# Expert loop of a gated attention and mixture-of-experts kernel: both groups of TensorE transposes put between the gate product and the linear product

## The chip, the cores and the metric

The kernel runs on one core of a Trainium2 chip. The metric is the device time of one execution in microseconds (us). The kernel before takes 871.43 us, the median of three runs (871.41 to 871.66). The profile is of one more execution, which took 875.14 us; its traced span is 873.4 us.

TensorE is called PE here, and its loading of the stationary operand PEld. VectorE is DVE, ScalarE is ACT, GpSimd is POOL, and SP issues plain loads and stores.

## The reference

The input has 8 sequences of 256 tokens with 512 features. Two residual steps are computed: a sigmoid attention against a context, and then a mixture of 16 experts, of which each token uses 4. All of it is float32.

```
x = x + tanh(g_xattn) * attention(layernorm(x), ctx, ctx)
x = x + tanh(g_ffn) * ffn(layernorm(x))

ffn:  t = rms_norm(x) * norm_w
      G = softmax over the 4 largest of (t @ gate_w.T + gate_b), zero elsewhere
      h = t @ w1[e].T + b1[e]                 # 512 -> 2 * 512, for each expert e
      a = min(h[even], 7);  b = clip(h[odd], -7, 7)
      act = a * sigmoid(1.702 * a) * (b + 1)
      y = act @ w2[e].T + b2[e]               # 512 -> 512
      out = x + sum over e of G[e] * y
```

## The kernel before, in words

The first stage, up to about 205 us, does the attention and the routing. It leaves the normed token rows in HBM (`t_rows`) and, for each expert, a list of its tokens with their gates. The expert loop then works through blocks of 128 listed rows. There are 75 blocks with the numbers 0 to 74; blocks 0 to 3 are written out in straight code, and blocks 4 to 74 run in the loops of `over_experts` (line 274). An expert has about five blocks. The change touches the loop's blocks alone.

For block `g` the work is this:

- POOL gathers the 128 rows from `t_rows` into `xg` (`gather`, line 463, indirect DMA on line 472). There is one `xg` for all loop blocks, so the gather waits until PE has turned the rows that were in it (`xt_mm`, line 469).
- PE turns the rows with four 128x128 transposes into the PSUM bank `ps_x` (`turn_rows`, line 1190; the transposes are on line 1187, in the helper `turn`).
- ACT copies `ps_x` to `xt_hi` (line 657) once PE has also finished the linear product of the block before, which still reads `xt_hi`; DVE writes the remainder to `xt_lo` (line 955).
- PE multiplies: `gate_product` (12 matmuls of 512 columns) and `linear_product` (12 more). Each operand is held as a high and a low part, hence three matmuls for each of the four slices of 128. All products have line 1211, in the helper `product`.
- ACT and DVE form the activated rows `hid` (DVE lines 980, 984, 989, 993, 996 and ACT line 673).
- PE turns `hid` into `ps_h` (`turn_hidden`, line 1200), ACT and DVE split it into `ht_hi` and `ht_lo` (lines 663 and 961), and PE does the third product (`down`, line 1215, 12 matmuls).
- DVE adds the bias (`y_sb`, line 968). POOL scales the rows by their gates (`y_out`, line 485) and adds them to the output by an indirect DMA (line 489).

The blocks overlap. In one pass of the loop with the number `g`, PE does the gate and linear products of block `g`, turns the hidden rows of block `g - 1`, turns the input rows of block `g + 1`, and does `down` of block `g - 1`. In one pass POOL scales and sends the rows of one block and then gathers the rows of a later one: `add_rows(before)`, `gather(g + 2)`. Its passes run one block behind those of PE, so the gather that a pass of PE needs is the last thing that POOL did, and it is issued behind the scaling (line 485) and the adding (line 489) of finished rows.

In the first three passes of each expert ACT and DVE also split the next expert's weights into high and low parts, two pieces of 1024 columns each pass: ACT line 563, DVE line 889 (`w_lo`). SP loads each piece of the raw weights as soon as its place is free.

The order on every engine is the order of the code; semaphores join the engines.

Of the kernel before, what the change touches and what calls it, by code (L numbers as in the profile page):

```python
# [43 lines left out]
def gated_attention_moe(nc, x, ctx_k, ctx_v, gates_in, norm_w, gate_wt, gate_b, w_cat, b_cat, out):  # L44
# [24 lines left out]
    with ExitStack() as ctx:  # L69
# [176 lines left out]
        def wait_past(eng, s, value):  # L246

            if not isinstance(value, int) or value > 0:
                eng.wait_ge(s, value)  # L249
# [6 lines left out]
        def rows_of(g):  # L256

            if not isinstance(g, int):
                return xg
            return xg_second if g in (1, 4) else xg_third if g == 2 else xg  # L260
# [841 lines left out]
        def _(pe):  # L1102
# [81 lines left out]
            def turn(dst, src):  # L1184
                for k in range(KT):
                    c = slice(k * P, (k + 1) * P)
                    ins = pe.transpose(dst[:, c], src[:, c], ident_r[:])  # L1187
                return ins

            def turn_rows(g):  # L1190
                if isinstance(g, int) and g in (1, 4):
                    pe.wait_ge(second_in, DMA * (1 if g == 1 else 2))
                elif isinstance(g, int) and g == 2:
                    pe.wait_ge(third_in, DMA)
                else:
                    pe.wait_ge(gathered, DMA * ({0: 1, 3: 2}.get(g, g - 2) if isinstance(g, int) else g - 2))
                wait_past(pe, xt_ready, g)
                turn(ps_x[:].bitcast(F32R), rows_of(g)).then_inc(xt_mm, 1)

            def turn_hidden(g):  # L1200
                pe.wait_ge(hid_ready, g + 1)
                pe.wait_ge(ht_ready, g + 1)
                turn(ps_h[:].bitcast(F32R), hid_r).then_inc(ht_mm, 1)

            def product(dst, hi, lo, wh, wl, col, step):

                n = 0
                for k in range(KT):
                    c = slice(col + k * step, col + k * step + 512)
                    for lhs, rhs in ((hi, wh), (hi, wl), (lo, wh)):  # L1210
                        ins = pe.matmul(dst[:], lhs[:, k, :], rhs[:, c], start=n == 0, stop=n == 3 * KT - 1)  # L1211
                        n += 1
                return ins

            def down(g, parity):
                pe.wait_ge(ht_ready, g + 2)
                wait_past(pe, y_ready, g)
                product(ps_y, ht_hi, ht_lo, w_hi[parity], w_lo[parity], W1COLS, H).then_inc(y_mm, 1)

            def gate_product(g, parity):  # L1220
                pe.wait_ge(xt_ready, g + 1)
                wait_past(pe, a_ready, g)
                product(ps_a, xt_hi, xt_lo, w_hi[parity], w_lo[parity], 0, 2 * I).then_inc(a_mm, 1)

            def linear_product(g, parity):
                wait_past(pe, b_read, g)
                product(ps_b, xt_hi, xt_lo, w_hi[parity], w_lo[parity], I, 2 * I).then_inc(b_mm, 1)

            def block(e, parity, g, before, first, share):
                if first:  # L1230
                    pe.wait_ge(hi_ready, NPW * e + NP1)
                    pe.wait_ge(lo_ready, NPW * e + NP1)
                gate_product(g, parity)
                turn_hidden(before)
                linear_product(g, parity)
                turn_rows(g + 1)
                down(before, 1 - parity if first else parity)
                if first:
                    pe.wait_ge(hi_ready, NPW * (e + 1))
                    pe.wait_ge(lo_ready, NPW * (e + 1))  # L1240
# [62 lines left out]
            turn_rows(4)  # L1303

            last = over_experts(pe, block)
            keep_clock_up(2)
            turn_hidden(last)
# [42 lines left out]
```

## Time and profile before

| | |
|---|---|
| median of the runs shown | 871.43 us |
| the profiled execution | 875.14 us, span 873.4 us |
| PE busy | 832.9 us, 95% of the span |
| DVE / POOL / ACT busy | 67% / 58% / 37% |
| granted PE clock, mean | 0.985 of full |
| chain of waits that ended last, PE's share | 73% |

The table is read from the top down: PE is busy nearly throughout, and the chain of work that ended last lies mostly on its matmuls. An average over the span does not say how much room there is before a transfer becomes late; that is read from single passes.

### The profile page before, as it was taken

The numbers are of one execution on the slowest core, as the hardware profiler recorded it, in microseconds if no ns is written. First come the engines' busy times: TensorE is split into PE (matmuls) and PEld (weight loads), VectorE is DVE, ScalarE is ACT, GpSimd is POOL, SyncE is SP. The second block draws the span as 40 slices with busy tenths as digits, with TensorE's granted clock in tenths as the row PEclk, the third lists the DMA queues.
The fourth block names the chain that finished last, engine by engine and source line by source line (L and its number), as shares of the span: only waits on it lengthen the run. The fifth ranks groups of instructions, "written<-read, shape, count | busy, mean of one in ns | idle before, by whom it ended". The sixth has DMA issues, their size and how long they took to land.

```text
span 873.4 us, 14819 instructions
## 1 busy us (share of the span) xinstructions
PE 832.9 (95%) x3836; PEld 639.6 (73%) x3837; DVE 582.0 (67%) x1137; ACT 320.4 (37%) x464; POOL 505.1 (58%) x523
## 2 busy tenths in 40 slices
PE   4999899988899999999999999999999999999994
PEld 2554455766788888888888888888888888888883
DVE  4465677675578677767768778585766858585652
ACT  3555576531243324233333433332332333332111
POOL 0033345654467666667666677676675757676563
PEclk9999999999999999999999999999999999999998
DMA  5653576517377676537667757474554747443323
GB/s 181 229 171 121 169 222 211 163 58 185 106 194 202 170 173 167 135 89 194 154 145 197 216 128 204 94 194 102 146 146 71 194 91 200 102 97 51 72 48 48
DMA packets 51077, 127.50 MB, mean 146 GB/s; under 512 B 8240, under 2 KB 12336, under 8 KB 51056
## 3 DMA queue, kind: packets, MB, share of 16 engines
q1 hardware_dynamic: 32048, 87.35, 30.3%
q0 software_dynamic: 19008, 39.93, 25.7%
q8 instruction: 7, 0.11, 0.0%
q14 instruction: 14, 0.11, 0.0%
HBM read 96.25 MB, written 31.00 MB: 146 GB/s over the span
## 4 chain that ended last, share of the span: by engine, by line
PE 73%; DMA 1%; issue 0%; POOL 0%; ACT 0%; DVE 0%; POOLq 0%; DVEq 0%; ACTq 0%
PE bank L1211 68%; PE bank L1187 5%; DMA xg<-t_rows,gather_idx 1%; PE bank L1247 0%; POOL out_rows L549 0%; ACT y_last L723 0%; DVE y_sb L968 0%; POOLq L452 0%; DVEq L249 0%; POOLq L552 0%; POOLq L548 0%; ACTq L722 0%
## 5 line engine op out<-in xcount | busy, mean ns | idle before, releaser
L663 ACT ACTIVATE ht_hi<-bank 128x512 fp32r<-128x512 f32 x75 | 44.9, 599 | 352.7 <-PE bank L1187 345.5
L485 POOL TENSOR_SCALAR y_out<-y_sb,add_gate 128x512 f32<-128x512 f32 x71 | 155.7, 2192 | 16.2 <-DVE y_sb L968 15.0
L489 POOL DMA_INDIRECT out_rows<-y_out,add_idx x73 | 119.6, 1638 | 64.6 <-POOL y_out L485 37.8
L472 POOL DMA_INDIRECT xg<-t_rows,gather_idx x72 | 86.0, 1195 | 74.3 <-issue 38.6
L1211 PE MATMUL bank<-w_hi_even,xt_hi 128*128 128x512 f32 x312 | 126.1, 404 | 2.2 <-DVE xt_lo L955 2.0
L439 POOL DMA_INDIRECT list_rows<-entry,place x64 | 64.6, 1010 | 108.7 <-DVE place L875 91.0
L1211 PE MATMUL bank<-w_hi_even,xt_lo 128*128 128x512 f32 x312 | 123.4, 395 | 0.0
L1211 PE MATMUL bank<-w_lo_even,xt_hi 128*128 128x512 f32 x312 | 122.5, 393 | 0.0
L961 DVE TENSOR_TENSOR ht_lo<-bank,ht_hi 128x512 fp32r<-128x512 f32 x75 | 51.9, 691 | 103.2 <-ACT ht_hi L663 103.1
L1211 PE MATMUL bank<-w_hi_odd,xt_hi 128*128 128x512 f32 x288 | 115.5, 401 | 1.1 <-DVE xt_lo L955 1.1
L1211 PE MATMUL bank<-w_hi_odd,xt_lo 128*128 128x512 f32 x288 | 113.0, 392 | 0.0
L1211 PE MATMUL bank<-w_lo_odd,xt_hi 128*128 128x512 f32 x288 | 112.2, 390 | 0.0
L984 DVE SCALAR_TENSOR_TENSOR up_b<-bank,bias 128x512 f32<-128x512 f32 x75 | 51.8, 691 | 69.7 <-PE bank L1211 65.1
L1116 PE MATMUL bank<-k_sb,q 128*128 128x512 f32 x128 | 61.4, 625 | 11.2 <-DMA k_sb<-in_ctx 7.9
L955 DVE TENSOR_TENSOR xt_lo<-bank,xt_hi 128x512 fp32r<-128x512 f32 x76 | 52.5, 691 | 27.5 <-ACT xt_hi L657 26.6
L1211 PEld LDWEIGHTS bank<-w_hi_even,xt_hi 128*128 128x128 f32 x312 | 59.1, 189 | 13.8 <-issue 2.6
L1211 PEld LDWEIGHTS bank<-w_hi_even,xt_lo 128*128 128x128 f32 x312 | 59.1, 189 | 13.3
L673 ACT ACTIVATE up_s<-up_a 128x512 f32<-128x512 f32 x75 | 47.4, 632 | 56.3 <-DVE up_a L980 56.3
L1211 PEld LDWEIGHTS bank<-w_lo_even,xt_hi 128*128 128x128 f32 x312 | 59.2, 190 | 11.5
L1211 PE MATMUL bank<-w_hi_even,ht_hi 128*128 128x512 f32 x156 | 64.8, 415 | 0.0
L657 ACT ACTIVATE xt_hi<-bank 128x512 fp32r<-128x512 f32 x76 | 45.5, 598 | 47.5 <-PE bank L1187 45.9
L1211 PEld LDWEIGHTS bank<-w_hi_odd,xt_lo 128*128 128x128 f32 x288 | 54.0, 188 | 12.1
(168 smaller groups left out, 1678.7 us busy)
## 6 DMA issues: line engine op xcount, KB each, us to landing
raw<-in_w SPq DMA_DIRECT2D x96, 512.0 KB
bias<-in_b SPq DMA_DIRECT2D x16, 768.0 KB
k_sb<-in_ctx SPq DMA_DIRECT2D x8, 512.0 KB, 3.8
v_sb<-in_ctx_t SPq DMA_DIRECT2D x8, 512.0 KB
t_rows<-t_sb SPq DMA_DIRECT2D x8, 512.0 KB
out_rows<-base SPq DMA_DIRECT2D x8, 512.0 KB
x_sb<-in_x SPq DMA_DIRECT2D x7, 512.0 KB
t_rows<-zeros SPq DMA_DIRECT2D x1, 2048.0 KB, 9.4
```

The source lines that it names most:

```text
L439: pool.indirect_dma_start(out=list_rows, out_offset=bass.IndirectOffsetOnAxis(ap=place[:, j, k:k + 1].bitcast(U32), axis=0), in_=entry[:, ...
L472: pool.indirect_dma_start(out=xg[:].bitcast(F32), out_offset=None, in_=t_rows, in_offset=bass.IndirectOffsetOnAxis(ap=gather_idx[:], axis= ...
L485: pool.tensor_scalar(y_out[:], y_sb[:], add_gate[:, 0:1], None, ALU.mult).then_inc(yo_ready, 1)
L489: pool.indirect_dma_start(out=out, out_offset=bass.IndirectOffsetOnAxis(ap=add_idx[:], axis=0), in_=y_out[:], in_offset=None, compute_op=A ...
L657: act.activation(xt_hi[:].rearrange("p k t -> p (k t)"), ps_x[:], ACT.Copy).then_inc(xt_hi_ready, 1)
L663: act.activation(ht_hi[:].rearrange("p k t -> p (k t)"), ps_h[:], ACT.Copy).then_inc(ht_hi_ready, 1)
L673: act.activation(up_s[:], up_a[:], ACT.Sigmoid, scale=ALPHA).then_inc(sg_ready, 1)
L955: dve.tensor_tensor(xt_lo[:].rearrange("p k t -> p (k t)"), ps_x[:], xt_hi[:].rearrange("p k t -> p (k t)").bitcast(F32), ALU.subtract).th ...
L961: dve.tensor_tensor(ht_lo[:].rearrange("p k t -> p (k t)"), ps_h[:], ht_hi[:].rearrange("p k t -> p (k t)").bitcast(F32), ALU.subtract).th ...
L984: dve.scalar_tensor_tensor(out=up_b[:], in0=ps_b[:], scalar=1.0, in1=bias[:, parity, I:2 * I], op0=ALU.add, op1=ALU.add).then_inc(b_read, 1)
L1116: ins = pe.matmul(ps_s[n % 3][:], q[:, j, n * P:(n + 1) * P], k_sb[:, j, :], start=j == 0, stop=j == J - 1)
L1211: ins = pe.matmul(dst[:], lhs[:, k, :], rhs[:, c], start=n == 0, stop=n == 3 * KT - 1)
```

## The change

In the loop's pass the four transposes of the next block's input rows move from behind the linear product to ahead of it. They then stand directly behind the four transposes of the hidden rows.

```
                 gate_product(g, parity)
                 turn_hidden(before)
+                turn_rows(g + 1)
                 linear_product(g, parity)
-                turn_rows(g + 1)
                 down(before, 1 - parity if first else parity)
```

Nothing else is changed: DVE, ACT, POOL and SP have the same instructions in the same order, and every wait stays with its instruction.

On PE before, this is the seam between the gate product and the linear product. `hid_r` is the hidden block, `w_hi`, `w_lo`, `xt_hi` and `xt_lo` are the two parts of the weights and of the turned input.

```order
L1211 MATMUL bank<-w_lo_even,xt_hi 128x512
L1211 MATMUL bank<-w_hi_even,xt_lo 128x512
L1187 MATMUL bank<-ident_r,hid_r 128x128 x4
L1211 MATMUL bank<-w_hi_even,xt_hi 128x512
L1211 MATMUL bank<-w_lo_even,xt_hi 128x512
```

Before, the gathered rows `xg` are turned behind the linear product; the register instruction belongs to the wait for the gather. `ht_hi` marks the start of `down`.

```order
L1211 MATMUL bank<-w_lo_even,xt_hi 128x512
L1211 MATMUL bank<-w_hi_even,xt_lo 128x512
L1196 REGISTER_ALU
L1187 MATMUL bank<-ident_r,xg 128x128 x4
L1211 MATMUL bank<-w_hi_even,ht_hi 128x512
L1211 MATMUL bank<-w_lo_even,ht_hi 128x512
```

After the change the first seam holds both groups, and the wait for the gather stands between them, ahead of the whole linear product.

```order
L1211 MATMUL bank<-w_lo_even,xt_hi 128x512
L1211 MATMUL bank<-w_hi_even,xt_lo 128x512
L1187 MATMUL bank<-ident_r,hid_r 128x128 x4
L1196 REGISTER_ALU
L1187 MATMUL bank<-ident_r,xg 128x128 x4
L1211 MATMUL bank<-w_hi_even,xt_hi 128x512
L1211 MATMUL bank<-w_lo_even,xt_hi 128x512
```

After the change nothing stands between the linear product and `down`.

```order
L1211 MATMUL bank<-w_lo_even,xt_hi 128x512
L1211 MATMUL bank<-w_hi_even,xt_lo 128x512
L1211 MATMUL bank<-w_hi_even,ht_hi 128x512
L1211 MATMUL bank<-w_lo_even,ht_hi 128x512
L1211 MATMUL bank<-w_hi_even,ht_lo 128x512
```

So 12 matmuls of 512 columns and one wait have changed places in each of the 71 passes of the loop, and the number of instructions is the same.

## Rows read from the trace of the kernel before

**Rows 1.** The page: chain that ended last, by line.
```profile
PE bank L1211 68%; PE bank L1187 5%; DMA xg<-t_rows,gather_idx 1%; PE bank L1247 0%; POOL out_rows L549 0%; ACT y_last L723 0%; DVE y_sb L968 0%; POOLq L452 0%; DVEq L249 0%; POOLq L552 0%; POOLq L548 0%; ACTq L722 0%
```

**Rows 2.** PE's waits: us in total, times, longest.
```profile
PE bank L1187 <- DMA xg<-t_rows,gather_idx: 2.5, 1, 2.5
```

**Rows 3.** Timeline of PE, one pass: start us, us, what, count.
```profile
439.10 0.46 PE L1187 MATMUL bank<-ident_r,xg 128*128 128x128 f32 x4
439.39 0.46 PE L1211 MATMUL bank<-w_hi_even,ht_hi 128*128 128x512 f32 x1
442.22 0.39 PE L1211 MATMUL bank<-w_hi_even,xt_hi 128*128 128x512 f32 x1
444.95 0.45 PE L1187 MATMUL bank<-ident_r,hid_r 128*128 128x128 f32 x4
445.24 0.46 PE L1211 MATMUL bank<-w_hi_even,xt_hi 128*128 128x512 f32 x1
448.09 0.46 PE L1187 MATMUL bank<-ident_r,xg 128*128 128x128 f32 x4
```

**Rows 4.** Timeline of PE ahead of the loop: `down` straight behind a linear product.
```profile
192.06 0.39 PE L1211 MATMUL bank<-w_hi_even,ht_hi 128*128 128x512 f32 x1
194.55 0.39 PE L1211 MATMUL bank<-w_hi_even,ht_lo 128*128 128x512 f32 x1
```

**Rows 5.** Timeline of PE ahead of the loop: the second of two groups of transposes.
```profile
180.34 0.51 PE L1187 MATMUL bank<-ident_r,xg_third 128*128 128x128 f32 x4
180.69 0.24 PE L1282 MATMUL bank<-carry,ones_r 128*128 128x16 f32 x1
```

**Rows 6.** Timeline of POOL in the pass of rows 3.
```profile
441.54 1.33 POOL L472 DMA_INDIRECT xg<-t_rows,gather_idx  x1 [0.81 <-issue]
```

**Rows 7.** Timeline of ACT and DVE in the same pass.
```profile
439.59 0.60 ACT L657 ACTIVATE xt_hi<-bank 128x512 fp32r<-128x512 f32 x1 [0.55 <-PE bank L1187]
441.28 0.69 DVE L993 SCALAR_TENSOR_TENSOR up_u<-up_s,up_b 128x512 f32<-128x512 f32 x1
442.01 0.69 DVE L996 SCALAR_TENSOR_TENSOR hid<-up_a,up_u 128x512 f32<-128x512 f32 x1
```

**Rows 8.** DMA in the window 444.8 to 445.0: POOL's queue, packets, MB, share.
```profile
q0 software_dynamic: 3, 0.00, 0.8%
```

**Rows 9.** Longest wait for a gather: chain, PE's timeline, DMA in 221.3 to 221.4.
```profile
213.43 8.26 DMA xg<-t_rows,gather_idx
...
216.33 0.46 PE L1211 MATMUL bank<-w_hi_even,xt_hi 128*128 128x512 f32 x1
221.74 0.54 PE L1187 MATMUL bank<-ident_r,xg 128*128 128x128 f32 x4 [2.45 <-DMA xg<-t_rows,gather_idx]
222.11 0.47 PE L1211 MATMUL bank<-w_hi_even,ht_hi 128*128 128x512 f32 x1
226.53 0.40 PE L1211 MATMUL bank<-w_hi_odd,xt_hi 128*128 128x512 f32 x1
...
q0 software_dynamic: 1, 0.00, 0.6%
```

**Rows 10.** Windows: busy us (x count) by engine, PE clock, DMA share, GB/s.
```profile
222.90:226.20 3.30, 3.30 (x9) 2.54 (x8) 2.41 (x4) 0.01 (x1) 1.11 (x2) 0.51 0.31 79
```

**Rows 11.** POOL's gathers and PE's hidden transposes, first and last of 43 close passes.
```profile
243.80 1.36 POOL L472 DMA_INDIRECT xg<-t_rows,gather_idx  x1 [0.83 <-issue]
247.23 0.29 PE L1187 MATMUL bank<-ident_r,hid_r 128*128 128x128 f32 x2
...
792.03 1.31 POOL L472 DMA_INDIRECT xg<-t_rows,gather_idx  x1 [0.81 <-issue]
795.42 0.29 PE L1187 MATMUL bank<-ident_r,hid_r 128*128 128x128 f32 x2
```

**Rows 12.** The same two for one of the 27 other passes.
```profile
620.15 1.02 POOL L472 DMA_INDIRECT xg<-t_rows,gather_idx  x1 [1.63 <-PE bank L1187]
624.68 0.29 PE L1187 MATMUL bank<-ident_r,hid_r 128*128 128x128 f32 x2
```

More of the change, by code:

```diff
@@ L1234, in block @@
                 turn_hidden(before)
+                turn_rows(g + 1)
                 linear_product(g, parity)
-                turn_rows(g + 1)
                 down(before, 1 - parity if first else parity)
```

## The prediction

> **What bounds the kernel now.** I read the chain of work that ended last first. It lies for 68% of the span on the products of line 1211 and for 5% on the transposes; a gather has 1% [rows 1]. The list of PE's waits comes next: in 70 of the 71 passes PE waits for no gather, and in one it waits 2.5 us [rows 2]. So PE sets the pace. The timeline of one pass gives it [rows 3]: gate product from 442.22, hidden transposes at 444.95, linear product at 445.24, row transposes at 448.09, and the same transposes one pass earlier at 439.10. A pass is 448.09 - 439.10 = 8.99 us. The question is what comes due earlier. The row transposes do: their place moves from 448.09 to about 445.24, by the 2.85 us of the linear product.
>
> **How close the gather is.** POOL issued this pass's gather from 441.54 to 442.87 [rows 6]. Its queue still moved packets in the window 444.8 to 445.0 and none after; narrowing the window puts the last one at 444.88 [rows 8]. From the issue's end to the landing are 2.0 us. The one long wait shows what follows: the last packet of that gather passed between 221.3 and 221.4 (narrowed: 221.33), and PE's transposes began at 221.74, so 0.41 us lie between landing and PE [rows 9]. The rows are thus usable at 444.88 + 0.41 = 445.29. Before, they are needed at 448.09: 2.8 us of room. After, they are needed at 445.24: none.
>
> I did the same for all gathers with a pass behind them, 70 beyond the long one. In 43 the place of the hidden transposes plus 0.29 us lies less than 0.5 us behind the landing (mean 0.26). The first and the last are [rows 11]: issue ends at 245.16 and 793.34, landings by narrowed windows at 247.27 and 795.37, transposes possible at 247.52 and 795.71. Over these the landing takes 1.9 to 2.3 us, mean 2.07. In the other 27 there is 0.9 us or more; [rows 12] has 624.68 + 0.29 against 623.19. The close ones are mostly the passes in which DVE also splits weights.
>
> **Does the room move with PE?** A wait only costs once if POOL runs freely, and each time if the gather is tied to PE. In the close passes the gather's end is 5.22 us ahead of the row transposes almost without exception. It takes 1.33 us there and 1.02 elsewhere [rows 6, 12], and ends 0.17 us behind the end of `hid` on DVE (442.70) [rows 6, 7]. I read this as POOL being held while DVE computes `up_u` and `hid`. Those follow ACT's copy to `xt_hi`, which began 0.20 us behind the row transposes before (439.39 to 439.59) [rows 3, 7]. After the change that copy follows the end of the linear product instead, because it waits for it too. Hence the gather's end stays 442.87 - 439.39 = 3.48 us behind the end of the last PE work ahead of `down`, whichever that is. A late PE makes the gather late, and the wait comes back in each close pass.
>
> The Trainium skill, page "Advanced Engine Details and Errata", section "GPSIMD Details", says that GpSimd shares a read and a write interface with VectorE and conflicts with VectorE instructions that have two SBUF inputs. That fits `up_u` and `hid`, which have two, and speaks for the tie; without it the gather would end after 1.02 us, 0.31 us earlier, which is the first rival below.
>
> **The sum, part by part.** Against the profiled execution's 875.14 us (span 873.4).
>
> 1. *Repeated wait, 43 passes.* Counted from the end of the linear product: gather ends at 3.48, lands at 3.48 + 2.07 = 5.55, usable at 5.96. PE gets there by `down` (2.72 to 2.84), gate (444.95 - 442.22 = 2.73) and hidden transposes (0.29) at 5.74 to 5.86. It waits 0.10 to 0.22 us. Then come 0.35 us of row transposes and 2.85 us of linear product: the pass takes 9.16 us against 8.99, +0.18. Times 43: +7.7. With landings of 1.9 and 2.3 us throughout it would be +0.5 and +17.6.
> 2. *Quiet passes, 27.* `down` loses the transposes in front of it. Behind transposes it takes 442.22 - 439.39 = 2.83 us [rows 3]; straight behind a linear product 12 matmuls take 2.49 / 11 x 12 = 2.72 [rows 4]. That gains 0.11. The second group of transposes costs 0.35 us instead of 0.29, since its first weight load no longer hides behind a long matmul [rows 5]: loses 0.06. Net -0.05, times 27: -1.4. Bounds: 0, and -0.12 if the second group costs nothing extra.
> 3. *The first pass of the loop.* The gather lands at 221.33 whatever PE does: it was issued long before, and it is the raw weights that it shares the DMA engines with. Before, the linear product ran from 216.33 to 219.1, ahead of that wait [rows 9]; it now comes behind it, +2.80. PE then idles from 216.33 to 221.74, 5.4 us instead of 2.6. After the 2.45 us wait the clock fell to half (0.51 of full in 222.9 to 226.2) and `down` took 226.53 - 222.11 = 4.42 us instead of 2.8 [rows 9, 10]. A longer idle time starts that stretch earlier at most; two matmuls more at 0.43 instead of 0.23 us make 0.3 to 0.4. I take +3.1. Bounds 2.8, and 5.2 if all twelve run at half clock.
> 4. *Nothing on the other engines.* DVE's linear rows start 0.3 us later in a pass, but into a gap of 0.2 to 0.3 us ahead of `xt_lo`; `xt_lo` is ready 1.5 us behind the linear product and the gate product needs it at 2.7. `hid` ends 3.3 us behind it and is needed at 5.5. If that cover went, each 0.1 us would cost 7 us over 71 passes; I cost it at 0.
>
> Sum: 7.7 - 1.4 + 3.1 = +9.4. The profiled execution would take 884.5, 3.7 us above its median as now: 871.43 + 9.4 = 880.8 us.
>
> **The rivals.**
>
> *No repeated wait (same).* POOL is not tied to `hid` but runs ahead once PE has been delayed. For it: the change moves `xt_mm` forward, for which POOL waits in the quiet passes [rows 12], and a pass 0.3 us longer puts `up_u` behind the gather's start; then the gather takes 1.02 us and the wait vanishes. Against: in the close passes the gather starts 0.26 us inside `up_u` [rows 6, 7], and a pass lengthened by 0.18 leaves it there. Only terms 2 and 3 would be left, with 70 quiet passes instead of 27: 3.1 - 3.5 to 3.1 - 1.4, that is 871.0 to 873.1, middle 872.1.
>
> *Faster.* The unbroken run of 36 matmuls is worth more than I allow: no penalty for the second group and 0.12 us gained in each of 70 passes, with landings early enough. It needs the landing to take under 1.85 us, or the tie to be gone. Time: -8.4 + 2.8 = -5.6, 865.8 us. It decides once the gain per pass exceeds 2.8 / 70 = 0.04 us with no waits. Against it stands the mean room of 0.26 us, less than the 0.41 us from landing to PE.
>
> *Later landings (slower still).* The landing takes longer when its packets meet others: the gather beside the first raw weights took 8.3 us from issue to landing [rows 9], and three or four of the quiet passes' had 2.3 to 2.5 us from its end. With 0.19 us more in each close pass the sum grows by 8.2: 889.0 us.
> The Trainium skill, page "DMA: Bandwidth & Descriptors", section "Anatomy of one DMA — SWDGE (gpsimd) path", gives about 2.0 us plus the bytes over 436 GB/s for a transfer issued by GpSimd. For the 256 KB of a gather that would be an estimate of 2.6 us; the trace has 2.0 to landing and 2.41 to PE's start. Counted from the end of the issue, the page would give this rival's time. By the trace alone it is the less likely.
>
> That the change does not do what it says is no rival: the order on PE shows the moved matmuls in every loop body.
>
> **How the numbers follow.** Forecast (tied gather, 880.8): 0.59, own range 875 to 886 from landings of 1.95 to 2.2 us. No repeated wait: 0.16. Faster: 0.11. Later landings: 0.14. A measurement of this kernel can tell about 0.2% (1.7 us) from no change. Faster holds the third case and a little of the second: 0.13. Same holds most of the second: 0.12. Slower holds the rest, 0.75. The range runs from 872, which keeps half of the second case, to 889.
>
> **What would show it.** In the changed kernel's list of PE's waits, line 1187 on the gather should have some 40 waits, 0.1 to 0.3 us each and 5 to 10 us together, besides one of 5.4 us that ends near 221.7. Passes in which weights are split should take 9.1 to 9.2 us, quiet ones 8.9 to 9.0. `down` should have 0.23 us behind its first matmul, and the gather should still end 0.17 us behind `hid`. The forecast is wrong if the close passes stay at 8.9 to 9.0 us, or if gathers there take 1.02 us.

## The result and the profile after

The changed kernel takes 882.60 us (median of five runs, 882.20 to 886.01); the kernel before took 871.43 us beside it. The ratio is 1.0125, with a 95% interval of 1.0106 to 1.0144: slower by some 11 us. The forecast was 880.8 us. The profiled execution of the changed kernel took 886.01 us (span 884.3), 3.4 us above its median, as that of before lies 3.7 above its own, so the two spans may be compared: 884.3 - 873.4 = 10.9 us.

The page and the list of PE's waits, to be read against [rows 1, 2]. A wait's row gives us in total, times, longest.

```profile
PE 836.7 (95%) x3836; PEld 646.2 (73%) x3837; DVE 583.3 (66%) x1137; ACT 320.1 (36%) x464; POOL 506.3 (57%) x523
PE bank L1211 6%; PE bank L1187 1%; DMA xg<-t_rows,gather_idx 0%; POOL out_rows L549 0%; PE bank L1247 0%; ACT y_last L723 0%; DVE hid L996 0%; DVE up_u L993 0%; DVE y_sb L968 0%; ACT xt_hi L657 0%; DVE up_b L989 0%; DVE xt_lo L955 0%; POOLq L279 0%; DVEq L249 0%; POOLq L552 0%
PE bank L1187 <- DMA xg<-t_rows,gather_idx: 7.3, 10, 3.9
```

The shares of this chain sum to 7%: it could be followed back over the last stretch alone, and its percentages are no measure. It still has one new thing in it: `hid`, `up_u` and `xt_hi` now stand on a chain that ends at PE. The waits for a gather have become ten: the long one of the first pass and nine more, 3.3 us together. But ten are not all. A wait of a few tenths disappears under the overlapping ends of the matmuls, so I read it as the distance from the hidden transposes to the row transposes. Without a wait that is 0.29 to 0.30 us. In 34 passes it is longer, by 9.85 us together.

One such pass on PE, to be read against [rows 3]: start us, us, what, count.

```profile
443.58 0.45 PE L1187 MATMUL bank<-ident_r,hid_r 128*128 128x128 f32 x4
444.09 0.55 PE L1187 MATMUL bank<-ident_r,xg 128*128 128x128 f32 x4
444.48 0.47 PE L1211 MATMUL bank<-w_hi_even,xt_hi 128*128 128x512 f32 x1
...
447.28 0.39 PE L1211 MATMUL bank<-w_hi_even,ht_hi 128*128 128x512 f32 x1
...
450.00 0.39 PE L1211 MATMUL bank<-w_hi_even,xt_hi 128*128 128x512 f32 x1
...
452.72 0.46 PE L1187 MATMUL bank<-ident_r,hid_r 128*128 128x128 f32 x4
453.15 0.53 PE L1187 MATMUL bank<-ident_r,xg 128*128 128x128 f32 x4
```

ACT, POOL and DVE ahead of its end, to be read against [rows 6, 7]:

```profile
447.54 0.60 ACT L657 ACTIVATE xt_hi<-bank 128x512 fp32r<-128x512 f32 x1 [0.88 <-PE bank L1211]
449.32 1.49 POOL L472 DMA_INDIRECT xg<-t_rows,gather_idx  x1 [0.81 <-issue]
449.23 0.69 DVE L993 SCALAR_TENSOR_TENSOR up_u<-up_s,up_b 128x512 f32<-128x512 f32 x1
449.95 0.69 DVE L996 SCALAR_TENSOR_TENSOR hid<-up_a,up_u 128x512 f32<-128x512 f32 x1
```

The loop goes round: the linear product ends near 447.28, ACT copies `xt_hi` behind it (its releaser is now line 1211 and no longer 1187), `hid` ends at 450.64, the gather at 450.81, 0.17 behind it, and 2.34 us later PE may turn the rows. From hidden transposes to hidden transposes the pass is 452.72 - 443.58 = 9.14 us.

A pass without a wait is 8.91 us on average (this one 8.88), and in it the three products stand close together (answers to [rows 4, 5]):

```profile
243.41 0.46 PE L1187 MATMUL bank<-ident_r,hid_r 128*128 128x128 f32 x4
243.71 0.51 PE L1187 MATMUL bank<-ident_r,xg 128*128 128x128 f32 x4
244.05 0.46 PE L1211 MATMUL bank<-w_hi_odd,xt_hi 128*128 128x512 f32 x1
...
246.85 0.39 PE L1211 MATMUL bank<-w_hi_odd,ht_hi 128*128 128x512 f32 x1
...
249.57 0.39 PE L1211 MATMUL bank<-w_hi_odd,xt_hi 128*128 128x512 f32 x1
```

`down` takes 249.57 - 246.85 = 2.72 us, and the second group of transposes 244.05 - 243.71 = 0.34.

The first pass of the loop, with the long wait (answers to [rows 9, 10]); the windows give busy us (x count) of PE, PEld, DVE, ACT, POOL, then PE's clock, DMA share and GB/s:

```profile
219.04 0.46 PE L1187 MATMUL bank<-ident_r,hid_r 128*128 128x128 f32 x4
223.44 0.75 PE L1187 MATMUL bank<-ident_r,xg 128*128 128x128 f32 x4 [3.94 <-DMA xg<-t_rows,gather_idx]
223.99 0.76 PE L1211 MATMUL bank<-w_hi_even,xt_hi 128*128 128x512 f32 x1
```
```profile
219.00:223.40 4.40, 0.50 (x5) 0.31 (x3) 1.29 (x2) 1.23 (x2) 0.00 (x0) 0.84 0.83 263
223.50:228.60 5.10, 5.10 (x15) 4.13 (x16) 0.00 (x0) 0.00 (x0) 1.55 (x4) 0.50 0.16 51
228.60:231.80 3.20, 3.20 (x14) 2.57 (x14) 2.48 (x5) 0.60 (x1) 0.00 (x0) 0.97 0.01 3
```

From the start of the hidden transposes PE does nothing else for 4.4 us, 3.94 of them listed as a wait. Then row transposes and linear product run at 0.50 of the full clock, the lower of its two levels (1.2 of 2.4 GHz).

All passes of the loop, measured from hidden transposes to hidden transposes (the first interval is the loop's first pass, the last, of 6.8 us, goes to the products behind the loop):

| | before | after |
|---|---|---|
| first interval | 13.32 us | 15.49 us |
| passes with a wait | none | 34, mean 9.23 us |
| passes without | 69 of 8.99 us | 35, mean 8.91 us |
| sum from first to last | 640.20 us | 648.06 us |

By kind: 34 x (+0.24) = +8.2 us, 35 x (-0.075) = -2.6, the first interval +2.2, the last +0.1. Together +7.9. The other 3 us of the span lie ahead of the loop, whose first hidden transposes come at 219.04 instead of 215.94. The change touches nothing there, and in the traces of the runs below this start lies anywhere between 211.8 and 218.8 us. So the trace shows 7.9 us that the change can have caused; the timed runs say some 11. A second trace of the changed kernel, at the end of the next section, has +7.4 in the loop and a start at 216.28. Where the other 3 us of the timed difference lie is not shown.

### The profile page after: what moved, and what is told of

Its sections match the earlier page's. It is cut to its first block and busy times, and to the rows that moved or that the text cites. A ratio compares the mean times of both kernels' runs of the same rounds, so it can differ in the third digit from the quotient of the medians.

```text
span 884.3 us, 14819 instructions
## 1 busy us (share of the span) xinstructions
PE 836.7 (95%) x3836; PEld 646.2 (73%) x3837; DVE 583.3 (66%) x1137; ACT 320.1 (36%) x464; POOL 506.3 (57%) x523
## 5 line engine op out<-in xcount | busy, mean ns | idle before, releaser
L485 POOL TENSOR_SCALAR y_out<-y_sb,add_gate 128x512 f32<-128x512 f32 x71 | 158.3, 2230 | 24.2 <-DVE y_sb L968 23.9
L1211 PEld LDWEIGHTS bank<-w_hi_odd,xt_hi 128*128 128x128 f32 x288 | 54.0, 188 | 11.6 <-issue 1.5
L1211 PEld LDWEIGHTS bank<-w_lo_odd,xt_hi 128*128 128x128 f32 x288 | 54.2, 188 | 10.1
```

The source lines that it names most:

```text
L485: pool.tensor_scalar(y_out[:], y_sb[:], add_gate[:, 0:1], None, ALU.mult).then_inc(yo_ready, 1)
```

## The experiments

My theory: of the 11 us about 3.5 come from the first pass of the loop and some 7 from gathers that are tied to PE through `hid`. What ties them is POOL's own work ahead of the gather, above all the scaling of `y_out`, which DVE holds up. Rivals: the new order costs something by itself, or the whole price is the first pass. All ratios are to the kernel before on the same chip; 0.001 is 0.87 us. There it took 872.51, 876.48 or 875.92 us, while the expectations reckon from 871.4; so their times are to be read as differences from that.

### The first pass alone, from both sides

```
-                turn_rows(g + 1)
+                late = isinstance(e, int) and e == 0
+                if not late:
+                    turn_rows(g + 1)
                 linear_product(g, parity)
+                if late:
+                    turn_rows(g + 1)
```

This is the changed kernel with the old order in the passes of expert 0. The traces show that this is the first pass of the loop alone: the next one already has the length of the other order.

> The changed kernel, but in the passes of expert 0 (the first of them is the one with the long wait for the gather) the row transposes stand behind the linear product as before. Theory 1 (three terms: the first pass costs about 2.2 to 3.1 us, some 34 passes wait again and again, the quiet ones gain 0.07 each): 2 to 3.5 us less than the changed kernel's 882.6, so 879.1 to 880.6. Rival (most of the loss sits in the first pass and the clock that falls behind it; the repeated waits are given back elsewhere): 872 to 875.

Measured: 878.96 us, ratio 1.0085 (1.0060 to 1.0111), which is +7.4 us. The first interval is 12.54 us, and 38 later passes have a wait, of 9.19 us on average. The loop of this trace is 644.87 us, +4.7, again some 3 us less than the timed runs say. By either measure most of the price is in the later passes.

The reverse, the kernel before with the new order in expert 0 alone (the same lines with `if late` and `if not late` exchanged):

> The kernel before, with the row transposes ahead of the linear product in expert 0's passes alone. Theory 1: only the first pass's term, +2 to +3.5 us: 873.5 to 875. Rival (the first pass costs nothing because the later start of the linear product is made up in the passes behind it): 871.4.

Measured: 879.22 us, ratio 1.0040 (1.0019 to 1.0061), +3.5 us. All passes but the first are 8.98 to 9.00 us. The first interval is 17.38:

```profile
217.96 0.46 PE L1187 MATMUL bank<-ident_r,hid_r 128*128 128x128 f32 x4
224.03 0.75 PE L1187 MATMUL bank<-ident_r,xg 128*128 128x128 f32 x4 [5.61 <-DMA xg<-t_rows,gather_idx]
```
```profile
218.40:223.40 5.00, 0.02 (x1) 0.00 (x0) 1.29 (x2) 1.23 (x2) 0.00 (x0) 0.97 0.94 307
223.70:229.00 5.30, 4.97 (x15) 4.00 (x16) 0.00 (x0) 0.00 (x0) 1.51 (x4) 0.50 0.18 49
```

Here the wait is about as long as the prediction gave it (5.61 us listed, 5.4 forecast), and the half clock covers the linear product behind it. The two runs add up to the whole of the change: 7.4 + 3.5 = 10.9 us. That they meet to the tenth is chance, since each is known to about 2 us only; by the plain medians they are 6.5 and 2.7.

### The gather ahead of the scaling

```
             def block(e, parity, g, before, first, share):
-                add_rows(before)
                 gather(g + 2)
+                add_rows(before)
```

In the changed kernel POOL issues the gather first and only then scales and adds.

> The changed kernel, but POOL issues the gather of a pass ahead of scaling and adding the finished rows, not behind. Theory 1: the gather lands some 5 us before it is needed, the 34 repeated waits (9.9 us in the profile, 8.2 us of longer passes) vanish and these passes become quiet ones of 8.91 us; left is the first pass: 882.6 - 8.2 - 34 x 0.07 = 872.0 (871 to 874). Rival (the second group of transposes and the changed timing on DVE lengthen the pass, the gather is only what the wait is booked on): 878 or more, with the time booked on another wait.

Measured: 879.93 us, ratio 1.0099 (1.0078 to 1.0119). In time, that missed. The passes show why: with few exceptions they are now 8.91 to 8.92 us, as the theory wants, but near 741 there are some of 11.56, 9.88, 9.12, 9.29 and 9.29 us. POOL, DVE and PE there:

```profile
741.61 0.18 POOL L480 CAST add_idx<-lists 128x1 uint32 x1 [4.20 <-DMA out_rows<-y_out,add_idx]
741.81 1.57 POOL L485 TENSOR_SCALAR y_out<-y_sb,add_gate 128x512 f32<-128x512 f32 x1
```
```profile
743.48 0.69 DVE L968 TENSOR_TENSOR y_sb<-bank,bias 128x512 f32<-128x512 f32 x1 [4.07 <-POOL y_out L485]
```
```profile
747.09 0.50 PE L1211 MATMUL bank<-w_hi_odd,ht_hi 128*128 128x512 f32 x1 [1.74 <-DVE ht_lo L961]
```

A gather that goes first pushes the adding late. POOL then waits for the DMA that adds the rows of the block before, DVE waits for POOL, and PE for DVE. The loop as a whole takes 643.00 us, +2.8 against before with a first interval of 16.49 (+3.2). Another 1.7 us lie behind the loop: from the last hidden transposes to the end of the span are 18.96 us instead of 17.21, and POOL waits 2.85 us for an adding to land ahead of the last scaling, where before it did not wait. Together that is less than the measured +8.6 us; where the rest lies one traced execution doesn't show.

Both edits together:

> Both of the above: the changed order on PE except in expert 0's passes, and POOL's gather ahead of the scaling. Theory 1: only the gain of the quiet pass is left, 70 x -0.07 = -5 us against the kernel before: 866.5 (865.5 to 868.5). Rival (the transposes together gain nothing, and 8.91 us in the quiet passes is made up elsewhere): 871.

Measured: 875.70 us, ratio 1.0027 (1.0006 to 1.0048); the same stretch, from 738.6, has 11.86, 10.12, 9.08, 9.33 and 9.27 us. Missed too: not faster, though 4.2 us below the run without the old order in expert 0. The expected gain is there, in 64 passes of 8.91 to 8.92 us, and these five passes, 5.1 us too long together, take it away again.

The gather first in the kernel before, where `down` is the last thing that PE does ahead of the next gate product:

> The kernel before, with POOL's gather ahead of the scaling and nothing else changed. Theory 1: there was 2.8 us of room, so an earlier gather is worth nothing: 871.4 (870.5 to 872.5). Rival (POOL's own order is what gains or costs, whatever PE does): 866 to 868 like the run with both, or slower than 873.

Measured: 974.38 us, ratio 1.119 (1.1167 to 1.1214). The expectation was wrong by 100 us. PE's longest waits are no longer for a gather, and POOL waits far more than before (39.2 us, 44 times) for the DMA that adds finished rows:

```profile
PE bank L1211 <- DVE ht_lo L961: 64.5, 36, 3.5
POOL add_idx L480 <- DMA out_rows<-y_out,add_idx: 178.7, 59, 4.9
```

The gather needs `xt_mm`, which the old order gives only behind the linear product. A gather placed first holds the scaling and adding of finished rows behind that, and 43 passes become longer, up to 15.4 us. I read this as the chain from `y_sb` through the scaling and the adding to the next scaling having become the bound; no run takes a link of it away. So moving the gather was a poor way to untie it: it trades one chain for another.

### Taking away what holds POOL

Two kernels leave POOL's order alone and shorten what it meets. In the first, DVE splits 64 of the 1024 columns of each weight piece in the loop and leaves out the low parts of the rest.

```
-                c = slice(k * PIECE, (k + 1) * PIECE)
+                c = slice(k * PIECE, k * PIECE + cols)
...
-                        split_lo(e + 1, 1 - parity, k)
+                        split_lo(e + 1, 1 - parity, k, 64)
```

> The changed kernel, in which DVE splits only 64 of the 1024 columns of each weight piece inside the loop; the rest of the low parts is left out. Theory 1: POOL's scaling is held by these splits; without them it takes 1.57 us, the gather is issued about a microsecond earlier in those passes, and the repeated waits vanish: 872 (870.5 to 873.5). Rival (the gather is late because its landing takes long, beside the raw weights, which are now asked for even earlier): the waits stay or grow, 880 or more.

Measured: 875.47 us, ratio 0.9988 (0.9967 to 1.0010). Three passes still have a wait, none above 9.13 us; the rest are 8.91. The same edit in the kernel before, since DVE's work by itself might be worth something:

> The kernel before with the same short splits on DVE. Theory 1: DVE is nowhere late in the order before, so nothing changes: 871.4 (870.5 to 872.5). Rival (the splits themselves cost PE time, by what they read and write): 868 or less, and then the run with short splits in the changed order must be read against this one.

Measured: 876.30 us, ratio 0.9987 (0.9964 to 1.0011), passes of 8.98 to 8.99 us. Without most of DVE's splits the two orders are equal in time: 11 us of difference have gone. In the traces the changed order still pays for the first pass (16.18 us against 13.00) and gets it back in the others, 8.91 against 8.99 us each.

In the second, POOL scales 64 of 512 columns and DVE splits as ever. The other 448 columns are sent as an older block left them, so this kernel does not compute the reference; it is there for its time alone.

```
-                    pool.tensor_scalar(y_out[:], y_sb[:], add_gate[:, 0:1], None, ALU.mult)
+                    pool.tensor_scalar(y_out[:, 0:64], y_sb[:, 0:64], add_gate[:, 0:1], None, ALU.mult)
```

> The changed kernel, in which POOL scales only 64 of the 512 columns of the finished rows; the other columns are sent unscaled from an older block. Theory 1: POOL reaches the gather 1.4 us or more earlier, the repeated waits vanish as with the gather first: 872 (870.5 to 874). Rival (the gather's end is fixed by DVE's hid whatever POOL does before it, so shortening POOL's own work changes nothing): 880 to 883.

Measured: 875.15 us, ratio 0.9995 (0.9975 to 1.0015); no pass has a wait. POOL in the changed kernel, in the one with short splits and in the one with short scaling:

```profile
443.25 2.55 POOL L485 TENSOR_SCALAR y_out<-y_sb,add_gate 128x512 f32<-128x512 f32 x1
```
```profile
445.48 1.57 POOL L485 TENSOR_SCALAR y_out<-y_sb,add_gate 128x512 f32<-128x512 f32 x1 [0.56 <-DVE y_sb L968]
450.57 1.02 POOL L472 DMA_INDIRECT xg<-t_rows,gather_idx  x1 [0.81 <-issue]
```
```profile
445.71 1.43 POOL L485 TENSOR_SCALAR y_out<-y_sb,add_gate 128x64 f32<-128x64 f32 x1
450.65 1.01 POOL L472 DMA_INDIRECT xg<-t_rows,gather_idx  x1 [0.81 <-issue]
```
```profile
451.44 0.69 DVE L993 SCALAR_TENSOR_TENSOR up_u<-up_s,up_b 128x512 f32<-128x512 f32 x1
```

About one microsecond less on POOL is enough. With the short scaling (the last two fences are that kernel) the gather begins 0.79 us ahead of `up_u` instead of 0.09 inside it, takes 1.01 us instead of 1.49, and lands in time. The scaling of 64 columns beside the splits still takes 1.43 us, hardly less than 512 columns take alone (1.57), and much more than the 0.45 us of 64 columns alone.

The traces show more of the tie than the prediction had. POOL is bound to DVE ahead of the gather, too. A scaling that runs beside the splits ends 1.36 to 1.44 us behind their end, in the kernel before as in the changed one, and the gather's start follows 3.5 us behind the scaling's end or later. The splits follow `hid` in DVE's order. So the start of a gather hangs on the `hid` of the pass before, and its end on the `hid` of its own pass. One thing on this way no run takes out: POOL also waits for the last adding to land before the next scaling, 47.2 us in 52 passes of the changed kernel against 39.2 in 44 before. How much of the lateness is due to that is not shown.

### The scaling on ACT

A version that computes all of the reference: ACT, 36% busy, scales at the end of its pass, and POOL only adds.

```
...
-                    pool.tensor_scalar(y_out[:], y_sb[:], add_gate[:, 0:1], None, ALU.mult).then_inc(yo_ready, 1)
...
+                act.wait_ge(gate_set, g)
+                act.wait_ge(added, DMA * (g - 1))
+                act.wait_ge(y_ready, g)
+                act.activation(y_out[:], y_sb[:], ACT.Copy, scale=add_gate[:, 0:1]).then_inc(yo_ready, 1)
```

> The changed kernel, but ACT and not POOL scales the finished rows (0.6 us on ACT at the end of its pass, where it idles), so POOL reaches the gather 1.6 to 3.4 us earlier; no work is left out. Theory 1: all passes but the first become 8.91 us, the first keeps its +2 to +4: loop of 631.5 us (hidden transposes of pass 4 to those of the last), 872 us, ratio to before 0.998 to 1.001. Rival (the gathers' landings are what is late): the repeated waits stay, ratio 1.006 or more.

Measured: 876.02 us against 875.92, ratio 1.0004 (0.9981 to 1.0027). All later passes but one (9.02) are 8.88 to 8.92 us. Behind the loop this kernel loses 1.2 us (18.38 us to the end of the span instead of 17.21). With the old order in expert 0:

> As the run before, and in expert 0's passes the row transposes stand behind the linear product as they used to. Theory 1: 70 passes of 8.91 instead of 8.99 us and no cost in the first: loop of 628 us against 633.4 of the kernel before, ratio 0.9935 to 0.996 (866 to 868 us). Rival (POOL falls behind once as it did with the gather first): 871 or more.

Measured: 872.34 us, ratio 0.9959 (0.9937 to 0.9981): faster than the kernel before by 3.6 us, the only version whose interval lies wholly on that side. Its later passes are 8.90 to 8.93 us but one of 9.12. Its POOL and ACT in one pass:

```profile
445.75 2.08 POOL L484 DMA_INDIRECT out_rows<-y_out,add_idx  x1 [1.88 <-ACT y_out L684]
447.29 0.75 POOL L468 CAST gather_idx<-lists 128x1 uint32 x1
448.85 1.00 POOL L472 DMA_INDIRECT xg<-t_rows,gather_idx  x1 [0.81 <-issue]
```
```profile
444.18 0.72 ACT L684 ACTIVATE y_out<-y_sb,add_gate 128x512 f32<-128x512 f32 x1 [2.47 <-DVE y_sb L967]
```
```profile
450.77 0.69 DVE L992 SCALAR_TENSOR_TENSOR up_u<-up_s,up_b 128x512 f32<-128x512 f32 x1
```

ACT takes 0.72 us for what held POOL for 2.55, and the gather ends 0.9 us ahead of `up_u`. One caution: the traced executions of these two kernels have the same span, 871.6 us, and first intervals of 15.47 and 15.63 us (in the second the gather was issued 1.4 us later and took 0.7 us longer). So the loop of the second is only 2.5 us shorter than that of the kernel before, not the 5.4 expected, and its first pass did not get shorter in this execution. What sets the two kernels apart, 0.0045 in the ratio, rests on twelve timed runs each and not on a trace. The control, the scaling on ACT in the old order:

> The kernel before with the scaling on ACT and nothing else changed. Theory 1: POOL's lateness costs nothing in the order before, so the passes stay at 8.99 us and the ratio at 0.999 to 1.001. Rival (the gain of the run before comes from the scaling and not from the order of the transposes): 0.996 or less.

Measured: 877.17 us, ratio 1.0017 (0.9997 to 1.0038), passes of 8.98 to 8.99 us. The scaling on ACT is worth nothing in the old order. Between this control and the last version lie 0.0058, or 5.1 us, with the scaling on ACT in both: that gain comes from the new order with its waits gone. It fits 69 passes that are 0.075 us shorter (5.2 us).

### The change once more

> The changed kernel once more, on the chip of the three runs before and against the same runs of the kernel before. Theory 1: 1.009 to 1.0125, with about 35 passes of 9.1 to 9.4 us. Rival (its first measurement was taken on a chip on which it was slow by chance): 1.005 or less.

Measured: 886.13 us, ratio 1.0115 (1.0091 to 1.0139). First interval 15.34 us, 36 passes with a wait, a loop of 647.63 us. The pattern of the first trace is no accident of one execution. The traced execution, 882.71 us, is the fastest of the six, so it can't tell where the 3 us lie that the loops lack.

## Why the prediction was right

**Term 1, the repeated wait: mechanism right, the size in part by luck.** Forecast were 43 passes of 9.16 us, +7.7. Measured were 34 of 9.23, +8.2. The count was too high by nine and the price of a pass too low, 0.18 instead of 0.24 us; the two errors nearly cancel. The page lists ten waits and not some 40, because the short ones only show in the distances. The tie to `hid` holds: in 31 of the 34 the gather ends 0.16 to 0.18 us behind `hid` and 3.53 us behind the end of the linear product (forecast 3.48), and its issue takes 1.07 to 1.54 us. In the second trace of the changed kernel 32 of 36 are tied so. From its end to PE's row transposes are 2.28 to 2.75 us, 2.45 on average, where the sum had 2.07 + 0.41 = 2.48. So the rows come at 5.98, as forecast (5.96); the mean wait of these 31 is 0.24 and not 0.10 to 0.22 because PE now gets to the place in 5.73 to 5.74 us, the lower end of my 5.74 to 5.86. The runs with short splits and short scaling show the cause: with the gather off `up_u`, at most three waits are left of 34.

Of the 43 close passes some escaped, and that is the first rival at work in part. I had it that a pass longer by 0.18 us would leave the gather's start inside `up_u`. In eight passes it did not stay there: the gather began between 0.12 us ahead of `up_u` and 0.02 behind its start, took its short time and ended 0.4 to 0.5 us ahead of `hid`. In six of the eight the pass before had waited 0.28 to 0.39 us. It is no strict rule: behind three other waits of 0.29 to 0.42 us the gather stayed just inside `up_u` and was held. One of the eight:

```profile
276.29 1.02 POOL L472 DMA_INDIRECT xg<-t_rows,gather_idx  x1 [0.82 <-issue]
```
```profile
276.38 0.69 DVE L993 SCALAR_TENSOR_TENSOR up_u<-up_s,up_b 128x512 f32<-128x512 f32 x1
277.11 0.69 DVE L996 SCALAR_TENSOR_TENSOR hid<-up_a,up_u 128x512 f32<-128x512 f32 x1
```

PE turned these rows at 280.17, 2.86 us behind the gather's end, without a wait. So a longer wait can free the next pass. Two passes went the other way: 10.00 and 9.88 us, with the gather's end 0.89 us behind `hid`.

The Trainium skill's page "Advanced Engine Details and Errata", section "GPSIMD Details", on the interface that GpSimd shares with VectorE, agrees with these traces, though it has no prices: the same gather takes 1.02 us ahead of `up_u` and 1.49 beside it, the same scaling 1.57 us and 2.55.

**Term 2, the quiet passes: right in sign, too small.** Forecast -0.05 us each; measured -0.075, 35 times, -2.6 instead of -1.4. `down` at 2.72 and the second group at 0.34 to 0.36 came as forecast. The rest is small change: the linear product takes 2.83 us on average instead of 2.85, and the second group 0.34 where I had 0.35. So -0.11 for `down`, +0.05 for the second group and -0.02 for the linear product. There were also 35 such passes and not 27.

**Term 3, the first pass: right in size by the timed runs, with the clock priced too low.** Forecast +3.1 us, bounds 2.8 and 5.2. The run with expert 0 alone measured +3.5 (1.7 to 5.3), its trace +4.1; the traces of the changed kernel have +2.2 and +2.0. Two more pairs of runs differ in this pass alone: changed kernel against first experiment 3.5 us, scaling on ACT with the new and with the old order in expert 0 3.9; a third, with the gather first, gives 6.3.

The term has two parts. The first is idle time. Counted as in the prediction, from the place of the linear product to the row transposes, it was 2.65 us in the trace before, 4.1 in the changed kernel and 5.8 with expert 0 alone, where 5.4 were forecast. The spread is the gather's: it shares the DMA engines with the raw weights, and its landing moves by more than a microsecond between executions.

The second part is the clock, and there the prediction was wrong twice. I took two more matmuls at half clock, 0.3 to 0.4 us. From the row transposes to the next hidden transposes the first pass took 1.7 us longer than the other passes before, 2.5 longer in the changed kernel and 2.7 with expert 0 alone: 0.8 to 1.0 us more, since all of the linear product ran at half clock. And my upper bound of 5.2 charged twelve matmuls in full without taking off the 1.6 us that `down` had already paid before; 2.8 + 2.4 - 1.6 = 3.6 would have been the bound. That the idle time of the changed kernel came out 1.3 us below the forecast hides this in its trace.

**Term 4, nothing elsewhere: right.** PE's waits for `xt_lo` and `hid` inside the loop do not grow, and quiet passes are shorter, not longer.

**The sum.** +9.4 forecast, +11.2 by the medians and +10.9 by the ratio. The terms measured in the trace, 8.2 - 2.6 + 2.2, give +7.9 with the last interval; in the timed runs of the two halves it is 7.4 + 3.5. So the forecast is close to the timed runs and 1.5 us above the loop of the trace, and the 3 us between these two are not placed.

**The other rivals.** *Faster* wanted the tie gone, and that was the right condition: with it gone by the scaling on ACT, and the first pass back in the old order, the order gains 3.6 us. It wanted 0.12 us per pass; 0.075 were there. *Later landings* did not occur as a rule: 2.45 us from the issue's end to PE is what the trace of before gave (2.41 and 2.48). The 0.19 us per pass that this rival added appear in no run. The Trainium skill's "DMA: Bandwidth & Descriptors", section "Anatomy of one DMA — SWDGE (gpsimd) path", gave an estimate of 2.6 us to the landing alone; the measured 2.45 includes PE's start.

## What to carry to other kernels

Before work is moved ahead of a transfer that it needs, ask from the profile not only how much room there is but what the transfer's start is tied to: a gather tied to the engine that it delays makes its wait come back in pass after pass. The cure was here not to move the gather but to shorten what its engine does ahead of it, or to put that on an idle engine. And what moves behind a long wait can be paid twice: by its own length, here 2.8 us, and by the lower clock behind the idle time, here 0.8 to 1.0 us.

## What the runs showed of the hardware

- A TensorE product that came behind a wait of 3.94 us ran at half clock: granted clock 0.50 from 223.5 to 228.6, 0.43 us per matmul of 512 columns instead of 0.23. Behind 5.61 us it was 0.50 from 223.7 to 229.0.
- POOL's scaling of 128x512 elements took 1.57 us alone and 2.55 beside DVE's weight splits; of 64 columns, 0.45 us alone and 1.43 beside them. Beside the splits a scaling ended 1.36 to 1.44 us behind their end. ACT took 0.72 us for the 512 columns.
- An indirect DMA's issue on POOL took 1.00 to 1.02 us, and 1.07 to 1.54 when DVE computed `up_u` and `hid` beside it; in 31 of the 34 passes with a wait it then ended 0.16 to 0.18 us behind `hid`.
- The gather put ahead of the adding in the kernel before cost 12%. There POOL waited 52.9 us in 29 passes for PE's transposes ahead of the gather and 178.7 us for the adding to land, and everything behind these waits on POOL was late.
